# Three dense graph layers: count products as two float32r matmuls on split rows, and block-wise output

## The reference

```python
def _L2(x, src, dst, deg):
    return jax.ops.segment_sum(x[src], dst, num_segments=n) / deg[:, None]

def _sage_conv(x, src, dst, inv_deg, W_self, W_neigh, b):
    agg = jax.ops.segment_sum(jnp.take(x, src, axis=0), dst, num_segments=n) * inv_deg[:, None]
    return x @ W_self + agg @ W_neigh + b
...
x = x + _L2(relu(layernorm(x)), src, dst, deg)
h = relu(layernorm(x))
h = relu(_sage_conv(h, src, dst, inv_deg, W_self1, W_neigh1, b1))
x = x + _sage_conv(h, src, dst, inv_deg, W_self2, W_neigh2, b2)
```

## Time and profile before

| | |
|---|---|
| median of 3 runs | 3104.72 us |
| profiled execution, first to last instruction | 3314.9 us |
| busy: TensorE matmul, VectorE, ScalarE, GpSimd | 76%, 68%, 29%, 25% |
| the norm ahead of the first dense layer to the end | 2795.5 to 3314.9 us |

### The profile page before, as it was taken

The page is one execution under the profiler, slowest core; times in us unless marked ns, Lnnn a source line. Parts: engine busy times, 40 slices in busy tenths (PEclk is TensorE's granted clock), DMA queues, the critical chain, the costliest instruction groups (busy, mean ns, idle before and its releaser), DMA issues. The chain is left out here.

```text
span 3314.9 us, 51871 instructions
## 1 busy us (share of the span) xinstructions
PE 2504.8 (76%) x12499; PEld 1548.3 (47%) x12613; DVE 2255.8 (68%) x10815; ACT 971.6 (29%) x2329; POOL 819.1 (25%) x856
## 2 busy tenths in 40 slices
PE   3663993888888787388867888788837884979898
PEld 2442881444444444266733444444425663444444
DVE  5666667778888888845686888888895446242223
ACT  1775990500000001133642000000012345333232
POOL 0000000066666665000004666665610000000000
PEclk8997996899999999699978999999968997999999
DMA  0001501388889886165426988888816543500100
GB/s 25 1 2 45 220 1 33 118 282 276 279 279 279 272 277 199 41 175 160 98 86 208 280 280 275 277 282 270 281 39 146 159 122 71 222 1 7 34 1 20
DMA packets 395805, 507.12 MB, mean 153 GB/s; under 512 B 29035, under 2 KB 331494, under 8 KB 394118
## 3 DMA queue, kind: packets, MB, share of 16 engines
q0 software_dynamic: 66560, 274.39, 25.0%
q1 hardware_dynamic: 327714, 227.61, 24.0%
q10 hardware_dynamic: 1252, 1.80, 0.2%
HBM read 409.08 MB, written 94.61 MB: 152 GB/s over the span
## 5 line engine op out<-in xcount | busy, mean ns | idle before, releaser
L939 POOL DMA_INDIRECT rows<-row_table,idx x832 | 794.6, 955 | 797.7 <-POOLq L134 306.7
L990 PE MATMUL z_ps<-xr,hot_ta 128*128 x2400 | 667.4, 385 | 245.7 <-DVE rows L1033 204.9
L1001 PE MATMUL z_ps<-rows,ident 128*128 128x256 f32 x1664 | 571.1, 425 | 4.6 <-issue 3.5
L990 PEld LDWEIGHTS z_ps<-xr,hot_ta 128*128 128x128 bf16 x2496 | 242.8, 97 | 545.6 <-issue 433.3
L2139 PE MATMUL dense_ps<-cnt,h 128*128 128x512 f32 (+1 forms) x1050 | 417.9, 556 | 86.4 <-ACT cnt L2097 82.7
L1033 DVE SCALAR_TENSOR_TENSOR rows<-rows,att_all 128x128 f32<-128x128 f32 x1664 | 421.8, 290 | 37.7 <-remote 20.8
L1059 DVE TENSOR_TENSOR rows<-z_ps,rows 128x256 f32<-128x256 f32 x832 | 348.8, 419 | 126.6 <-PE z_ps L1001 92.1
L1033 DVE SCALAR_TENSOR_TENSOR rows<-z_ps,att_all 128x128 f32<-128x128 f32 x1664 | 411.4, 282 | 21.6 <-issue 21.2
L1376 PE MATMUL acc_m<-xr,hot_m 128*128 x1984 | 342.0, 293 | 73.2 <-issue 54.2
L1376 PEld LDWEIGHTS acc_m<-xr,hot_m 128*128 128x128 f32 x1984 | 284.1, 195 | 138.0 <-issue 132.7
L1017 ACT COPY side<-side_ps 128x96 f32<-128x96 f32 x104 | 24.9, 239 | 1044.8 <-remote 813.1
(11 more groups left out here) (399 smaller groups left out, 3149.7 us busy)
## 6 DMA issues: line engine op xcount, KB each, us to landing
xr<-kept_rows SPq DMA_DIRECT2D x124, 512.0 KB
kept_rows<-rows SPq DMA_DIRECT2D x416, 128.0 KB
spread_a<-rel_rows SPq DMA_DIRECT2D x208, 128.0 KB
counts_line<-counts SPq DMA_DIRECT2D x1, 19550.0 KB
counts<-counts_line SPq DMA_DIRECT2D x6, 3200.0 KB
rows<-row_table,idx POOLq DMA_INDIRECT x832
row_table<-xl_ring SPq DMA_DIRECT2D x50, 258.0 KB
rows<-row_table SPq DMA_DIRECT2D x32, 320.0 KB
```

Source lines behind the costliest of these rows:

```text
L939: nc.gpsimd.indirect_dma_start(out=rows[:, u, :], out_offset=None, in_=table, in_offset=bass.IndirectOffsetOnAxis(ap=c.idx[:, n:n + 1], ax ...
L990: nc.tensor.matmul(ps[:, n % Z, :], hot, tile[:, m, 0:HC], start=m == 0, stop=False, skip_group_check=True)
L1001: nc.tensor.matmul(ps[:, n % Z, HALF_C:HC], c.ident[:, :], rows[:, n % ROWS, HALF_C:HC], start=False, stop=True, skip_group_check=True).th ...
```

## The change

Each float32 row block is written as the sum of two float32r parts: `parts[0]` is the row rounded to float32r, `parts[1]` what is left. Each count product becomes two float32r matmuls into the same sum, one for each part, with the counts cast to float32r. A count over 4095 would not be exact in that format. As edges are sorted by destination, only the node that holds edge 0, 4096, 8192, ... (13 of them, `PEAKS`) can have such counts. `gated_layer` therefore takes these nodes' columns apart: the high bits go to 16 extra columns (two extra windows of the saved table, made by GpSimd and VectorE), the low 12 bits replace the column's counts in the saved table, by 13 small patches from SP. Each dense layer sums the extra columns with its first chunk, splits the sums, and adds them to the right column of each chunk with one more product against a 0/1 matrix that GpSimd makes (`fix`).

With it come: the chunk of 53 nodes is taken first; `FIX = 8`, `finish` moves from step 12 to 17, `turn` from 4 to 11, `result` from 18 to 21, and `copy_sums` from 7 to 11; `sum_t` and `h_t` have one buffer; the sage weights are loaded within their layer; the norms ahead make the two parts (5 copies on ScalarE, 5 subtractions on VectorE); the second norm saves x to `x_line`, since its room is used in the sage layers; the middle layer writes two tables and both are loaded back; the last layer loads x by blocks, adds, and stores the output by blocks, in place of the phase at the end.

```diff
+PEAK = 1 << 12
+PEAKS = -(-E // PEAK)
+PEAK_WINDOWS = 2
+PEAK_COLS = PEAK_WINDOWS * W_NODES
...
+        if parts is not None:
+            for n, tiles in enumerate(groups):
+                dve.wait_ge(s["high"], n + 1)
+                nc.vector.tensor_tensor(out=parts[1][:, tiles, :], in0=out[:, tiles, :],
+                                        in1=parts[0][:, tiles, :].bitcast(F32), op=ALU.subtract)
...
+            for tiles in groups:
+                if tiles.stop <= ACT_TILES:
+                    act.wait_ge(s["rows"], tiles.stop)
+                else:
+                    act.wait_ge(s["rest"], 1)
+                nc.scalar.copy(parts[0][:, tiles, :], out[:, tiles, :]).then_inc(s["high"], 1)
...
-        sp.dma_start(counts_line[:, :, :], counts[:, 1:1 + WINDOWS, :]).then_inc(s["saved"], 16)
-        sp.wait_ge(s["saved"], 16)
+        sp.dma_start(peak[0:1, NODE, 0:PEAKS], bass.AP(dst.tensor, dst.offset, [[0, 1], [PEAK, PEAKS]]),
+                     allow_slow_non_contiguous=True).then_inc(s["peaks"], 16)
+        sp.dma_start(counts_line[:, 0:WINDOWS, :], counts[:, 1:1 + WINDOWS, :]).then_inc(s["saved"], 16)
+        sp.wait_ge(s["high"], 1)
+        sp.dma_start(counts_line[:, WINDOWS:WINDOWS + PEAK_WINDOWS, :], high_w).then_inc(s["saved"], 16)
+        sp.wait_ge(s["saved"], 2 * 16)
+        for j in range(PEAKS):
+            sp.wait_ge(s["low"], j + 1)
+            if j > 0:
+                sp.wait_ge(s["patched"], 16 * j)
+            window, = peak_values(WINDOW, j, 1, mybir.EngineType.SP, (WINDOWS - 1) * W_COLS)
+            sp.dma_start(bass.AP(counts_line.tensor, window, [[(WINDOWS + PEAK_WINDOWS) * W_COLS, P],
+                                                              [1, W_COLS]]), low_w[:, j % RINGS, :])\
+              .then_inc(s["patched"], 16)
+        sp.wait_ge(s["patched"], 16 * PEAKS)
...
+        for j in range(PEAKS):
+            column, = peak_values(COLUMN, j, 1, mybir.EngineType.Pool, WINDOWS * W_COLS + W_NODES - 1)
+            nc.gpsimd.tensor_copy(
+                high_w[:, j // W_NODES, j % W_NODES::W_NODES],
+                flat[:, bass.ds(column, W_COLS)].rearrange("p (k d) -> p k d", d=W_NODES)[:, :, 0])\
+              .then_inc(s["columns"], 1)
+        for j in range(PEAKS):
+            place, = peak_values(PLACE, j, 1, mybir.EngineType.Pool, WINDOWS * W_COLS)
+            if j >= RINGS:
+                pool.wait_ge(s["patched"], 16 * (j - RINGS + 1))
+            nc.gpsimd.tensor_copy(low_w[:, j % RINGS, :], flat[:, bass.ds(place, W_COLS)])\
+              .then_inc(s["windows"], 1)
...
+        def split_high():
+            dve.wait_ge(s["columns"], PEAKS)
+            nc.vector.tensor_single_scalar(high_w, high_w, (1 << 16) - PEAK, op=ALU.bitwise_and)\
+              .then_inc(s["high"], 1)
+        def split_low(j):
+            dve.wait_ge(s["windows"], j + 1)
+            mine = low_w[:, j % RINGS, :]
+            nc.vector.tensor_single_scalar(mine, mine, PEAK - 1, op=ALU.bitwise_and).then_inc(s["low"], 1)
...
+                if n == 5:
+                    find_peaks()
+                if n == NODE_TILES:
+                    split_high()
+                if n > NODE_TILES and n % 4 == 0 and (n - NODE_TILES) // 4 < PEAKS:
+                    split_low((n - NODE_TILES) // 4)
...
+    rest = len(whole) - 1
+    chunks = [(rest, whole[rest][0], whole[rest][1])] + [(q, low, size) for q, (low, size) in enumerate(whole[:rest])]
+    LAST = len(chunks) - 1
...
+    FIX = 8
...
+        for o in range(len(chunks)):
+            n = fix_step(o)
+            pool.wait_ge(s["used"], n - BUFS + 1)
+            nc.gpsimd.tensor_scalar(cnt[0:PEAK_COLS, n % BUFS, 0:width(o)], columns[:, 0:width(o)],
+                                    own_node[:, o:o + 1], None, ALU.is_equal).then_inc(s["cast_p"], 1)
...
+        def both(to, left, right, first, last):
+            nc.tensor.matmul(to, left[0], right, start=first, stop=False, skip_group_check=True)
+            return nc.tensor.matmul(to, left[1], right, start=False, stop=last, skip_group_check=True)
...
+                last = both(ps[:, TURNED, o % 2, t % T * P:(t % T + 1) * P],
+                            [part[:, t, :] for part in parts], c.ident_r[:, :], True, True)
...
+        def fix(o):
+            n = fix_step(o)
+            if o == 0:
+                pe.wait_ge(s["high"], 1)
+                pe.wait_ge(s["low"], 1)
+            pe.wait_ge(s["cast_p"], o + 1)
+            both(ps[:, SUM, o % 2, 0:width(o)], [part[:, :] for part in peak_t],
+                 cnt[0:PEAK_COLS, n % BUFS, 0:width(o)], False, True).then_inc(s["used"], 1)
...
+                last = both(ps[:, SUM, o % 2, 0:columns_of(o)], [part[:, k, :] for part in parts],
+                            cnt[:, n % BUFS, 0:columns_of(o)], k == 0, False)
                 last.then_inc(s["used"], 1)
-                if k == 4 and sage is not None:
-                    turn(q)
-                if k == 12 and q > 0:
-                    finish(q - 1)
-        finish(len(chunks) - 1)
+                if k == 2 and o == 1:
+                    turn_peaks()
+                if k == FIX and o > 0:
+                    fix(o - 1)
+                if k == 11 and sage is not None:
+                    turn(o)
+                if k == 17 and o > 0:
+                    finish(o - 1)
+        fix(LAST)
+        finish(LAST)
...
+        def copy_sums(o):
+            act.wait_ge(s["used"], fix_step(o) + 1)
+            if o >= 1:
+                act.wait_ge(s["prod"], o)
+            else:
+                act.wait_ge(s["zeros"], 1)
+            nc.scalar.copy(sum_t[:, 0:width(o)], ps[:, SUM, o % 2, 0:width(o)]).then_inc(s["sum_t"], 1)
...
+                    act.wait_ge(s["turned"], o + 1)
+                    if o >= 1:
+                        act.wait_ge(s["prod"], o)
+                    size = len(tiles_of(o)) * P
+                    nc.scalar.copy(h_t[:, 0:size], ps[:, TURNED, o % 2, 0:size]).then_inc(s["h_t"], 1)
...
+        def peak_nodes():
+            dve.wait_ge(s["nodes_in"], 2 * 16)
+            first, before = nodes[:, 0:1], nodes[:, 1:2]
+            link(nc.vector.tensor_copy(nodes[:, :], nodes_i[:, :]))
...
+            if tables is not None and o >= 1:
+                dve.wait_ge(s["stored"][0], 16 * o)
+                dve.wait_ge(s["stored"][1], 16 * o)
...
+                high = extra[:, 0, 0:n * P]
+                link(nc.vector.tensor_scalar(to, to, 0.0, None, ALU.max))
+                link(nc.vector.tensor_copy(high.bitcast(F32R), to))
+                nc.vector.tensor_tensor(out=extra[:, 1, 0:n * P].bitcast(F32R), in0=to, in1=high,
+                                        op=ALU.subtract).then_inc(s["res"], 1)
             else:
-                to = x[:, tiles[0]:tiles[-1] + 1, :]
-                nc.vector.tensor_tensor(out=to, in0=to, in1=out, op=ALU.add).then_inc(s["res"], 1)
-        for q in range(len(chunks)):
+                dve.wait_ge(s["x_in"][at], 16 * (o // 2 + 1))
+                nc.vector.tensor_tensor(out=to, in0=to, in1=extra[:, at, 0:n * P], op=ALU.add)\
+                  .then_inc(s["res"], 1)
...
+                if k == 21 and o > 0:
+                    result(o - 1)
...
+        sp.wait_ge(s["zeros"], 2)
+        for at in range(2):
+            sp.dma_start(nodes_i[at:PEAKS, at:at + 1], bass.AP(dst.tensor, dst.offset, [[PEAK, PEAKS - at], [1, 1]]),
+                         allow_slow_non_contiguous=True).then_inc(s["nodes_in"], 16)
...
+                    for k, table in enumerate(tables):
+                        sp.dma_start(table[tiles[0] * P:(tiles[-1] + 1) * P, :]
+                                     .rearrange("(t p) c -> p t c", p=P),
+                                     extra[:, k, 0:len(tiles) * P]
+                                     .rearrange("p (t c) -> p t c", c=C)).then_inc(s["stored"][k], 16)
+                    continue
+                if o == 0:
+                    sp.dma_start(out[NODES_FULL * P:N, :], res[0:NODES_REST, 0, 0:C])\
+                      .then_inc(s["stored"][0], 16)
+                else:
+                    sp.dma_start(out[tiles[0] * P:(tiles[-1] + 1) * P, :].rearrange("(t p) c -> p t c", p=P),
+                                 res[:, o % 2, 0:len(tiles) * P].rearrange("p (t c) -> p t c", c=C))\
+                      .then_inc(s["stored"][o % 2], 16)
+                if o + 2 < len(chunks):
+                    load_x(o + 2)
...
+norm_relu(nc, c, x, h, add=h, parts=parts)
+first.close()
+c.ident_r = sb("ident_r", [P, P], F32R)
+counts = sb("counts", [P, WINDOWS + PEAK_WINDOWS, W_COLS], U16)
+dense_layer(nc, c, counts, parts, inv_deg, x, dst, counts_line=counts_line)
+with nc.sbuf_tensor(fresh(nc, "h_whole"), [P, NODE_TILES, C], F32) as whole:
+    def keep_x(sp, sem):
+        sp.dma_start(x_line, x[:, :, :].rearrange("p t c -> p (t c)")).then_inc(sem, 16)
+        return 1
+    norm_relu(nc, c, x, whole, loads=keep_x, parts=parts)
```

(10 more changed lines are left out.)

325 lines of the change are left out of this document (199 added, 126 removed).

## The result

The changed kernel takes 2992.12 us (median of four runs, 2988.12 to 2993.83) where the kernel before takes 3104.81 (3103.32 to 3107.38): a ratio of 0.9637, with an interval of 0.9623 to 0.9651, or 112.7 us less. The forecast was 2962, so 143 less, with a range of 2938 to 3004. The direction and the mechanism came out as forecast; a fifth of the gain was missing, and most of what follows asks where it went.

The account below looks back on a forecast made before the run. Dense layers bound by TensorE's float32 product rate; layer savings -152.9, norms +7, reload +5.6, tables and memsets +2, end -6, gated layer +1 give -143 us: 3104.7 to 2962, range 2938 to 3004.

Parts of the forecast that it names:

- Rival 1: Dense layers' products: float32r no faster, 0.429 us per matmul, steps stay 0.857; +33 us, 3138; 7 in 100.
- Rival 2: Dense layers' products: weight loads don't hide, 0.12 us added per matmul, steps of 0.67; 3045 us; 6 in 100.
- Rival 4: Gated layer: chain of GpSimd and SP holds VectorE; 2982 us and more if a gather exceeds 3.5 us; 7 in 100.
- Rival 5: Dense layers: casts become the bound, so TensorE doesn't gain; a ScalarE pair costs 0.62 plus 0.1; 2 in 100.
- rival 3: Dense layers' extras weigh more: narrow matmuls +11, GpSimd +9, low clock +9; 2962 to 2991; part of forecast's range.
- the signs of being wrong: Profile after: records 0.33 or 0.43 apart, clock below 1.00 in big chunks, or ScalarE idle in the gated layer.
- The matmul, taken at 0.215: Dense layers' products: each float32r matmul of 512 columns 0.215 us, step 0.43; products fall 64.2 us per layer.
- If TensorE's lighter load there keeps the clock down into the big chunk, +3 a layer; I take none.: Small first chunk of the dense layers, at clock 0.50: possible +3 us a layer in the big chunk; none counted.
- The fix, 0.43 and a wait of 0.5: Each dense layer: fix's two matmuls at 0.43 us, +2.8 a layer; TensorE waits 0.5 for GpSimd six times, +3.1.
- The result's waits, 9.5 + 5: TensorE waiting behind VectorE's result, five chunks each: +9.5 us in the middle layer, +5 in the last.
- The turns, norms, reload and end: Turns +2.9 us per sage layer; two norms +7 together; reload between sage layers +5.6; final store -6.
- The expected lengths of the layers (92, 113, 108 us): Sign in the profile after: dense layers of about 92, 113 and 108 us where there were 153, 156 and 156.

Follow-up runs that it names:

- the halved loads: Changed kernel with wide chunks' products loading 64 of 128 weight columns, except each chunk's first step; half the sums missing: 2988.63 us, measured once.
- the bfloat16 run: Changed kernel with the first dense layer's parts, counts and extra columns' operands in bfloat16 in place of float32r: 2985.34 us, measured once.
- the wide matmuls ahead: Changed kernel plus twelve float32r matmuls of 512 columns ahead of each dense layer's small chunk: 3182.85 us, ratio 0.9662 to the kernel before.
- the run that holds the clock: Changed kernel with GpSimd's own buffer, result in pieces, twelve wide matmuls before the small chunk and one after every second narrow step: 3164.62 us.
- the two edits: Changed kernel with GpSimd's 0/1 matrix in its own buffer and VectorE's result issued in pieces between casts: 3161.82 us, ratio 0.9589 to the kernel before.

## Why the prediction was right, and where it was off

The mechanism held at each of its steps: the product of 512 columns was the bound, two float32r matmuls replace it at about half its time, VectorE's result and GpSimd's matrix become waits, the gated layer does not. Rival 1 (no faster product) would have cost 33 us by the forecast; with the old rate put in for the products, it costs 38 to 41. Rival 2 (weight loads not hidden) falls with the pitch of 0.233, and with the halved loads that all but leave it; a load is longer than the 0.12 us estimated (188 ns, and 194 in the kernel before), but it hides. Rival 4 falls with the gated layer's 0.9 us. Rival 5 is 54 us away, behind another halving of TensorE's work. Of rival 3's three parts one came, the low clock (9 forecast, 8.6 measured below); the narrow matmuls and GpSimd's 1.55 us were as in the forecast's own sum. That its total of 2991 is so near is luck, since the two other misses, the rate and the fix's own length, stood in no rival. Of the signs of being wrong one was there in part: the clock is below 1.00 for the first 4.2 to 5.0 us of wide products in each layer.

The 30 us between forecast and result, by the sum's own terms:

- **The matmul, taken at 0.215.** 0.2334 in the first layer and 0.235 in the others, 300 to a layer: 5.5 + 6 + 6 = 17.5 us. The upper bound was so far away that I took the bfloat16 row; it is that row's form that the bfloat16 run confirms, at 0.2161. The Trainium skill (FP8 and Floating Point Precision, TensorE Precision Notes) has true float32 as four passes and names a reduced precision beside it; taking that for one pass of the four gave an estimate of 0.214, and the measured 0.2334 decides, 9% above.
- **"If TensorE's lighter load there keeps the clock down into the big chunk, +3 a layer; I take none."** It does keep it down. The small chunk's steps were put at 0.24 us, from a row at clock 1.00, though the same paragraph has them at 0.50; they take 0.43: 12.2 and 11.8 us in the two sage layers in place of 7.3, so +4.9 and +4.5. In the first layer only some 2 us of it show, as the next chunk's load lands 33.9 us after the norm's start and holds the rest (with the wide matmuls ahead, whose small chunk takes 9.0 us, the wide products start at 35.2 us, in place of 37.3). Against that, the wide steps at the low clock lose 1.4 to 1.7 us a layer (from the run that holds the clock), where I had left the 3 us of before: some -3 over two layers. Together +8.6.
- **The fix, 0.43 and a wait of 0.5.** The wait is 0.38 by the period. The fix is 0.85: in the trace of the two edits, with no wait, the matmul ahead of it starts at 2829.33, the two of the fix at 2829.65 and 2830.00, the next two at 2830.31 and 2830.65, so 1.32 us for four starts, of which two would take 0.47 without it. 18 x (1.23 - 0.93) = +5.4.
- **The result's waits, 9.5 + 5.** 8.3 + 4.7 by the periods: -1.5.
- The turns, norms, reload and end: within half a microsecond each of the forecast.

That makes 17.5 + 8.6 + 5.4 - 1.5 = 30.0, against 30.3 missing, with some 2 us of uncertainty in the measurement itself. The match is closer than the parts allow: the 3.5 us that the low clock costs at the ends of the sage layers are not among them, so that smaller terms, not worked out one by one, must have come some 3 us below the forecast. The expected lengths of the layers (92, 113, 108 us) were each short by 8 to 12 us for these reasons.

Scaling the saving to the unprofiled time would have been wrong for the reason given: the layers span the same on a chip where the rest takes 190 us longer.

## What to carry to other kernels

When a step that bounds a stage is halved, cost everything that its old length covered, by order rather than by buffers: what stands ahead of the next urgent instruction on the same engine is a stall that no further buffer removes, and issuing it in pieces between the urgent ones does. Work that is narrow for TensorE is not cheap at the start of a stage: it ran at half clock here and brought nothing for the stretch behind it, and wide work put ahead of it gained 2 us where TensorE would have idled and nothing where it had to wait for that work. A short wait can go with a cost beyond its length: with one or both of them gone, the clock held to the end of a layer, which was worth another 3.5 us, and with TensorE's work halved again the clock fell in the middle of it. And a rate for a data type that the trace doesn't show needs a range of its own in the sum: 0.018 us was the largest single miss, because it stood there 900 times.

## What the runs showed of the hardware

- float32r matmuls of 512 columns start 0.2334 us apart at a granted clock of 1.00 and 0.4265 at 0.50 (1.2 GHz). The bfloat16 ones start 0.2161 apart at 1.00 and 0.427 at 0.50. So at the low clock the four-byte form costs nothing extra (one column a cycle at 1.2 GHz would be 0.427), and at the high one it takes 8% more than the bfloat16 form.
- A weight load of 128 columns takes 188 ns in four bytes, one of 64 columns 134, and one of 16 rows by 128 columns 182 to 185. The Trainium skill (TensorE: Matmul & The Clock Gate, LDWEIGHTS) says that it goes by columns and not by rows; the traces agree in that. Its formula gives an estimate of 107 ns for 128 columns; measured are the 188 above, and 98 in bfloat16.
- Around the fix, whose weights have 16 rows, each start is 0.31 to 0.35 us behind the one before in place of 0.233. The first product behind float32 matmuls of 128 columns, with weights of 128 rows, takes 0.32 too, so the change of rows is not shown to be the cause.
- The clock fell with TensorE at work: 3 us into matmuls of 72 columns, after 5 us of wide ones (one wait, of 0.30 us); in another layer it held for 6 us of the same. The Trainium skill (TensorE: Matmul & The Clock Gate, Part 1) ties the low clock to idleness; here the records, which overlap, show TensorE busy for 3.00 of each 3 us at 0.50.
- GpSimd's comparison of 512 four-byte columns takes 1.55 us. The Trainium skill's 769 ns for a tight loop (GPSIMD Engine Reference, 3.1) isn't reached. VectorE's casts take 0.55 us while it runs, in place of 0.43.
- The split of the counts at 4096 is the kernel's own choice (`PEAK`); no run here looks at where counts stop being exact in float32r.
